# A decoder layer on one core: three stages of the attention steps in another order

## The reference

```python
qkv = x @ W_qkv
ret = einsum('bhtd,bhsd->bhts', q, k) * decay
r = einsum('bhts,bhsd->bhtd', ret, v) + cross
x = layernorm(x + group_norm(r))
# cross attention, q from x, k and v from the context
scores = where(causal, einsum('bhqd,bhkd->bhqk', q, k) * scale, -inf)
x = layernorm(x + (softmax(scores) @ v) @ Wo.T + bo)
# experts
probs = softmax(x @ router_w.T); two largest, renormed
x = layernorm(x + sum_e combine_e * (gelu(x @ w_fc[e] + b_fc[e]) @ w_proj[e] + b_proj[e]))
```

## Time and profile before

| | |
|---|---|
| median of 3 runs | 986.08 us (985.74 to 988.63) |
| span of the profiled execution | 984.6 us |
| PE busy / PEld busy | 923.6 us (94%) / 821.1 us (83%) |
| DVE busy / ACT busy / POOL busy | 663.6 us (67%) / 607.6 us (62%) / 381.9 us (39%) |
| mean granted TensorE clock | 0.979 |

### The profile page before, as it was taken

The page is one execution under the profiler, slowest core; times in us unless marked ns, Lnnn a source line. Parts: engine busy times, 40 slices in busy tenths (PEclk is TensorE's granted clock), DMA queues, the critical chain, the costliest instruction groups (busy, mean ns, idle before and its releaser), DMA issues.

```text
span 984.6 us, 29858 instructions
## 1 busy us (share of the span) xinstructions
PE 923.6 (94%) x10845; PEld 821.1 (83%) x10845; DVE 663.6 (67%) x1977; ACT 607.6 (62%) x1531; POOL 381.9 (39%) x639
## 2 busy tenths in 40 slices
PE   6899999999999999999987999999999999999950
PEld 4788888888888888888777999999999999999950
DVE  4577787777877877877744677575755775665536
ACT  4556656656556666666556566576765675665536
POOL 0224554555544656555524422222222223222223
PEclk9999999999999999999989999999999999999985
DMA  8111141111111111113012552523434433523228
GB/s 280 50 34 57 61 142 45 56 56 66 56 46 44 63 59 61 51 54 110 29 34 50 120 139 44 139 45 67 120 57 130 100 83 57 131 43 48 43 48 325
DMA packets 57361, 79.90 MB, mean 81 GB/s; under 512 B 5728, under 2 KB 46048, under 8 KB 57120
## 3 DMA queue, kind: packets, MB, share of 16 engines
q1 hardware_dynamic: 41504, 58.50, 18.1%
q0 software_dynamic: 13536, 18.16, 10.6%
q10 hardware_dynamic: 2208, 1.73, 0.6%
HBM read 52.10 MB, written 29.71 MB: 83 GB/s over the span
## 4 chain that ended last, share of the span: by engine, by line
PE 79%; ACT 7%; DVE 5%; issue 4%; DMA 2%; SPq 1%; POOL 1%; ACTq 0%; another core or an unknown queue 0%; DVEq 0%; POOLq 0%
PE bank L828 16%; PE bank L842 11%; PE bank L511 11%; PE bank L844 5%; PE bank L647 4%; PE bank L673 4%; PE bank L573 3%; PE bank L718 3%; PE bank L694 3%; PE bank L626 3%; PE bank L598 3%; PE bank L593 2%; ACT h_f L1171 2%; PE bank L732 2%; ACT last_out L1243 1%
## 5 line engine op out<-in xcount | busy, mean ns | idle before, releaser
L828 PE MATMUL bank<-xs_hi,w_both 128*128 128x256 f32 x1152 | 242.2, 287 | 1.3 <-DVE xs_lo L1471 0.8
L1165 ACT ACTIVATE h_parts<-bank,bfc_s 128x256 fp32r<-128x256 f32 x288 | 139.9, 486 | 154.6 <-PE bank L828 150.5
L1721 POOL DMA_INDIRECT residual_sum<-y_w,meta_i x72 | 114.6, 1591 | 299.6 <-DVE y_w L1543 275.7
L1501 DVE TENSOR_TENSOR h_parts<-h_f,h_parts 128x256 fp32r<-128x256 f32 x288 | 121.4, 426 | 140.2 <-ACT h_f L1171 136.6
L842 PE MATMUL bank<-w_both,h_parts 128*128 128x512 f32 x544 | 200.0, 398 | 1.1 <-DVE h_parts L1501 1.1
L828 PEld LDWEIGHTS bank<-xs_hi,w_both 128*128 128x128 f32 x1152 | 191.5, 190 | 9.4 <-issue 1.6
L828 PE MATMUL bank<-xs_lo,w_both 128*128 128x256 f32 x576 | 162.9, 283 | 0.0
L844 PE MATMUL bank<-w_both,h_parts 128*128 128x256 f32 x544 | 153.1, 281 | 0.0
L1171 ACT ACTIVATE h_f<-bank,bfc_s 128x256 f32<-128x256 f32 x288 | 139.4, 484 | 3.9 <-DVE h_parts L1501 3.4
L842 PEld LDWEIGHTS bank<-w_both,h_parts 128*128 128x128 f32 x544 | 102.5, 188 | 20.0 <-DVE h_parts L1501 4.0
L828 PEld LDWEIGHTS bank<-xs_lo,w_both 128*128 128x128 f32 x576 | 109.7, 191 | 0.0
(11 more groups left out here) (186 smaller groups left out, 2138.2 us busy)
## 6 DMA issues: line engine op xcount, KB each, us to landing
rows<-sent_rows SPq DMA_DIRECT2D x37, 258.0 KB
xc_raw<-in_turned SPq DMA_DIRECT2D x32, 256.0 KB, 3.0
w_raw<-in_w_fc SPq DMA_DIRECT2D x8, 1024.0 KB
w_raw<-in_w_proj SPq DMA_DIRECT2D x8, 1024.0 KB
x_t<-in_x SPq DMA_DIRECT2D x32, 128.0 KB, 2.2
residual_sum<-x_row SPq DMA_DIRECT2D x32, 128.0 KB, 1.7
last_in<-residual_sum SPq DMA_DIRECT2D x7, 512.0 KB, 7.8
result<-last_out SPq DMA_DIRECT2D x7, 512.0 KB, 2.7
```

Of the source, the lines that this page charges most:

```text
L828: last = mm(ps_h(g, j), w[:, at:at + P], v[:, k, :], start=(n == 0), stop=(n == 3 * NCH - 1))
L1165: A(h_hi[j % 4][:, :], ps_h(g, j), ACT.Gelu_apprx_tanh, bias=bias)
L1501: V.tensor_tensor(h_lo[j % 4][:, :], h_f[j % 2][:, :], h_hi[j % 4][:, :].bitcast(f32), ALU.subtract).then_inc(s["h_split"], 1)
L1721: G.indirect_dma_start(total, bass.IndirectOffsetOnAxis(meta_i[:, half:half + 1], 0), y_w[:, half, :], None, compute_op=ALU.add)\
```

## The change

Three engines' lists are written in another order; no stage is changed, added or dropped.

```diff
--- before.py
+++ after.py
@@ -751,16 +751,16 @@
                     run(ret_scores, At(k))
                     run(att_back, At(k - 3))
                     run(x1_turn, At(k - 1))
-                    pair_run(prep_kx, k // 2)
+                    run(att_proj, At(k - 3))
                     run(qx, At(k - 1))
-                    run(att_proj, At(k - 3))
                     run(att_scores, At(k - 2))
                     run(ret_values, At(k))
                     run(rank, At(k - 4))
-                    run(max_scores, At(k - 1))
+                    pair_run(prep_kx, k // 2)
                     run(gn_mean, At(k))
                     run(y_back, At(k))
                     run(x2_turn, At(k - 3))
+                    run(max_scores, At(k - 1))
                     run(att_values, At(k - 2))
                     run(logits, At(k - 3))
                     run(prep_v, At(k + 1))
@@ -785,8 +785,8 @@
                         fc0(0)
                     run(gn_mean, At(k))
                     run(y_back, At(k))
+                    run(x2_turn, At(k - 3))
                     run(max_scores, At(k - 1))
-                    run(x2_turn, At(k - 3))
                     run(att_values, At(k - 2))
                     run(logits, At(k - 3))
                     run(prep_v, At(k + 1))
@@ -1090,7 +1090,6 @@
                     if k >= 0:
                         pair_run(x_high, (k + 2) // 2, 0)
                     run(att_back_out, At(k - 3))
-                    pair_run(kx_out, k // 2)
                     run(max_out, At(k - 2))
                     run(qx_out, At(k - 1))
                     for r in range(0, 2):
@@ -1098,6 +1097,7 @@
                     for r in range(2, 4):
                         run(att_exp, At(k - 2), r)
                     run(y_out, At(k))
+                    pair_run(kx_out, k // 2)
                     run(x2_T_out, At(k - 3))
                     run(o_out, At(k - 2))
                     run(v_out, At(k + 1))
@@ -1405,17 +1405,17 @@
                     run(put, At(k - 4))
                     run(ln2_norm, At(k - 3))
                     run(gn_moments, At(k))
+                    run(gn_centre, At(k))
                     for r in range(NT):
                         run(att_max, At(k - 1), r)
-                    run(max_twice, At(k - 1))
-                    run(gn_centre, At(k))
                     run(lg_out, At(k - 3))
                     run(ln1_stats, At(k))
+                    run(max_twice, At(k - 1))
+                    run(ln1_sum, At(k))
                     run(att_norm, At(k - 2))
-                    run(ln1_sum, At(k))
-                    run(pick, At(k - 3))
                     run(ln1_norm, At(k))
                     run(max_split, At(k - 1))
+                    run(pick, At(k - 3))
                 if odd:
                     for r in range(NT):
                         run(ret_decay, At(k), r)
```

## The result

The changed kernel takes 1032.26 us (median of 4 runs, 1028.52 to 1033.45) beside 986.93 us of the kernel before (985.74 to 988.63): a ratio of 1.047, with a 95% interval of 1.045 to 1.049. It is slower by 45.3 us. The forecast was 1025.4 us, in a range of 1008 to 1036.

What follows compares the result with a forecast made beforehand. The loop through VectorE's decay, which releases TensorE in every step, was taken as the bound. Even steps 14.5 x 2.15 = 31.2 us plus odd steps 13.5 x 0.6 = 8.1 us, together 39.3, gave 1025.4 us, range 1008 to 1036.

Steps and rivals of the forecast that it cites:

- The loop: Decay, attention scores, retention values, query-major scores, maxima, norms, next decay: lateness in it lengthens the 30.06 us pair.
- rival 3: TensorE's own work is the bound; the even steps' 0.42 us stall becomes pure gain, 979.8 us; chance 0.04.
- Odd steps, 0.6 us: Second norm's turn waits for VectorE's rank count (L1372); query-major scores, maxima and next decay 0.6 us later, bounds 0.2 and 0.7.
- Even steps, first part, 1.42 us for the maxima: Projection behind the retention values delays the query-major scores, so the maxima start at 231.13, 1.42 us later.
- The front was a tie: Even steps: retention values at 226.39 by TensorE's front, 226.43 by the decay, so the front costs and frees nothing.
- Even steps, second part, the split's wait of 1.0 us: With the pick behind it, VectorE's split waits 1.0 us for ScalarE's rounded maxima (L1039).
- Rival 1: The split doesn't wait for ScalarE: even term 1.13 instead of 2.15 us, 1010.6 us; chance 0.15.
- 2.15 was the term: Even steps: the next decay ends at 241.01, 2.15 us later than before; 14.5 times makes 31.2 us.
- half an even term: Step 2 counted as half of a full even step's 2.15 us, as it has half of the pipeline.
- half an odd term: Step 31 counted as half of an odd step's 0.6 us.
- rival 2: New TensorE waits lower the clock to 0.94 over attention's 460 us: 1035 to 1053 us; chance 0.08.
- step 2 has half of the pipeline: Term of the sum: besides 14 full even steps, 4 to 30, step 2 counts half, giving 14.5 x 2.15 = 31.2 us.

Runs made afterwards that it cites:

- decay_later: Kernel before, with VectorE's even steps making the low part of the context in front of the four decays instead of behind them: 1000.2 us, ratio 1.013.
- both_early: Kernel before, with the pick behind the next step's decays and, in odd steps, ScalarE's rounding of the maxima ahead of the turned-back attention copy: 985.6 us, ratio 0.997.
- pick_after_decay: Kernel before, with VectorE's pick moved in every step from the step's end to behind the next step's decays: 987.8 us, ratio 1.002.
- kx_front: Changed kernel, with the context key projection and its copy back in the even step's front, the second norm's turn still ahead of the scores: 1023.9 us, ratio 1.038.
- kx_behind_only: Kernel before, with projection and copy moved behind retention values and rank, output ahead of query projection; VectorE's lists and the turn left alone: 1004.0 us, ratio 1.018.
- pick_back: Changed kernel, with VectorE's pick put back in front of the first norm's output and the split in even steps: 1015.6 us, ratio 1.028.
- max_hi_first: Changed kernel, with ScalarE's rounding of the maxima ahead of the turned-back attention copy and second row copy in odd steps: 1012.0 us, ratio 1.026.
- after_old_start: Changed kernel, with the old lists for steps -1 to 3 on all three engines: 1027.3 us, ratio 1.040.
- split_projection: both_early with the context key projection cut in halves, one in the even step's front, one behind the rank, its copy behind the group's sums: 980.2 us, ratio 0.991.
- even_only: Changed kernel, with TensorE's odd list undone, so only the even steps' lists of three engines are changed: 1023.5 us, ratio 1.037.
- odd_turn_only: Kernel before, with only the second norm's turn put ahead of the query-major scores in odd steps: 997.6 us, ratio 1.010.

## Why the prediction was right, point by point

**The loop.** Right in what it was used for, and too strong in its words. A decay that comes later is paid in full (0.82 of 0.85 us in decay_later). But "the decay on VectorE releases TensorE in every step" holds only for the odd steps; there both_early brings the decay 0.3 us forward and the retention values and the step's end with it. In the even steps decay and TensorE's own front came out within 0.14 us of each other, which pick_after_decay shows with 2.62 us in place of 1.62 and no gain. The equal 1.63 and 1.62 of the earlier trace rows were a bound in one kind of step and a tie in the other, and no row that I laid out could tell them apart. Rows that I left out could. The attention scores of the kernel before, in the steps 13 and 14:

```profile
208.47 1.31 PE L673 MATMUL bank<-qx_own,kxT 32*128 32x256 f32 x15
...
224.11 1.27 PE L673 MATMUL bank<-qx_own,kxT 32*128 32x256 f32 x16
```

In the odd step the retention values start 210.44 - 208.47 = 1.97 us behind them, in the even step 225.83 - 224.11 = 1.72: only the odd step's scores are held up, by 0.25 us. My rival 3 (979.8 us) used the same distances as its point of decision; it fell, since nothing the change does brings the front and the decay forward together.

**Odd steps, 0.6 us.** Measured 0.72 us a pair; the wait for L1372 is there with 0.34 us before each turn. The handoff that I put at "some hundredths" is the difference: the turn starts 218.84 - 218.69 = 0.15 us behind the end of VectorE's row.

**Even steps, first part, 1.42 us for the maxima.** The front was a tie as laid out: TensorE waits 1.26 us for ScalarE's copy, and the retention values start 247.06 - 245.44 = 1.62 us behind the decay. The scores start 250.78 - 245.44 = 5.34 us behind the decay's end, 5.51 were laid out (229.72 - 224.21). The mean follows 1.51 us behind the projection's start as laid out; the projection starts 3.13 instead of 3.20 us behind the decay, and the scores 0.70 instead of 0.80 us behind the mean. The maxima start 6.75 us behind it, 6.92 laid out.

What I had wrong is whose 1.51 us these are. I priced the projection as work that the loop must carry. In kx_front it is not there, TensorE waits 1.18 us for the group's sums at the same place, and the pair is only 0.08 us shorter. I never laid out when these sums are ready. The size came out because the projection is hardly longer than the wait that it covers, and that was luck: the moved scores, which now stand behind the mean, cost this first microsecond with or without the projection. The projection costs it only when the scores stand right behind it, as in kx_behind_only.

**Even steps, second part, the split's wait of 1.0 us.** Measured 1.16 us, in 13 of 13 pairs. Rival 1 is out by pick_back, which cuts this wait to 0.41 us, and max_hi_first, which ends it; they give back 1.00 and 1.14 us a pair. From one decay's end to the next it is 262.18 - 245.44 = 16.74 us, 2.09 more than before; 2.15 was the term.

**What was missing.** 2.81 us a pair against 2.75 explains 0.8 of the 7.5 us by which the span was too short. Of the rest, 2.3 are the later first start, which the order has no part in (last section). To the steps 0 to 4 I had given half an even term for step 2 (1.1 us) and of step 4 the 1.05 us by which TensorE's next step starts later, 2.1 together; they took 5.9, so 3.7 are missing there. To the stretch behind step 31 I had given 1.4 us, half an odd term and the split's wait of step 30; it took 2.0, so 0.6 are missing. In the first steps the order made the difference, as after_old_start shows, and the granted clock was lower there. The windows of the kernel before and then of the changed one, from 10 to 20, 20 to 35 and 35 to 50 us (length, busy by engine, clock, DMA share, GB/s):

```profile
10.00:20.00 10.00, 7.34 (x58) 6.36 (x57) 2.95 (x5) 4.48 (x10) 0.00 (x0) 0.90 1.06 367
20.00:35.00 15.00, 11.68 (x171) 9.90 (x170) 7.43 (x16) 6.38 (x17) 5.20 (x10) 1.00 0.33 100
35.00:50.00 15.00, 13.08 (x238) 10.88 (x237) 8.14 (x20) 8.84 (x23) 3.10 (x7) 1.00 0.03 10
```

```profile
10.00:20.00 10.00, 7.47 (x33) 6.85 (x32) 1.96 (x3) 3.51 (x6) 0.00 (x0) 0.50 1.06 358
20.00:35.00 15.00, 11.67 (x125) 9.62 (x124) 6.96 (x15) 5.38 (x14) 5.26 (x10) 0.85 0.32 95
35.00:50.00 15.00, 12.72 (x167) 10.35 (x171) 9.54 (x21) 7.85 (x22) 3.08 (x7) 0.83 0.07 21
```

That is rival 2 in a small way: not in the steady steps, whose clock stayed at 1.00, but in the first ones. A lower clock comes with such a loss also where the projection stays in front: both_early, at 0.93 and 0.85 in the last two of these windows, takes 69.5 us from the first retention scores to step 5, while pick_after_decay, with the same list for TensorE, and split_projection, which has all moves of both_early, take 64.9 and 64.6 at 1.00. So how the missing 3.7 us divide between the new waits and the clock is open. The term of the sum that was mis-sized is "step 2 has half of the pipeline": it gave the steps 0 to 3 1.1 us, and they took 4.7. The 2.0 us behind the start of step 31 come with a clock of 0.85 between 519 and 575 us, where the kernel before had 0.94 in its drain; they are within what this stretch varies from run to run, and their cause stays open.

## What to carry to other kernels

In a software pipeline written out by hand, a full TensorE row says nothing about slack: set the starts of one stage beside the ends of its inputs, step by step, and follow the loop. Equal distances mean either a bound or a tie: look whether the stage that waits is itself drawn out, and let a run that makes the input earlier and one that makes it later tell which. A stage that looks like filler may be the cover of a wait on another engine, and when it is moved, the wait comes out where it stood; where it goes it is paid again, unless a wait stands there that it can cover. Before a moved stage is priced, look up when the inputs of the stage behind it are ready. Count the first and last steps of a pipeline apart, since a cover that is spare in the steady state may be the only one there.

## What the runs showed of the hardware

*The start.* Up to 17 us all these kernels run the same list, and yet the first retention scores start either at 17.7 to 17.9 us (the kernel before, both_early, even_only, kx_behind_only) or at 19.6 to 20.3 us (the changed kernel and the eight others). TensorE's pace makes the difference. In the early group the second and third block of twelve projection matmuls (L511, 256 columns) take 0.13 us from one matmul to the next, in the late group 0.23 us. Two blocks of twelve at 0.1 us each are the 2.3 us. The windows from 12 to 15 us of the kernel before and of odd_turn_only hold the same twelve matmuls:

```profile
12.00:15.00 3.00, 1.68 (x12) 1.48 (x12) 0.00 (x0) 1.10 (x3) 0.00 (x0) 0.98 1.04 366
```

```profile
12.00:15.00 3.00, 2.70 (x12) 2.63 (x12) 0.00 (x0) 0.24 (x1) 0.00 (x0) 1.00 1.04 364
```

The changed kernel has the slow pace with a granted clock of 0.50 in this window, the 1.2 GHz level. odd_turn_only has the same pace, and its clock is given as 1.00. So this column can't be trusted in the first microseconds of a profile; the pace of equal matmuls can. Both groups hold kernels of both orders (even_only and kx_behind_only in the early one, odd_turn_only and pick_after_decay in the late one), so the 2.3 us at the start are no effect of the order.

*The end.* From the start of step 31 on, where nearly all instructions stand in the same order in all of them, it takes 505.3 to 512.3 us to the end. So the 2.0 us at the end need not be an effect of the order. The four runs of the changed kernel, whose times go from 1028.52 to 1033.45 us, have mean clocks from 0.973 down to 0.965.

*Waits and the clock.* In the steady steps of the changed kernel TensorE had a wait of 1.3 us in each even step and kept 1.00 throughout. What made the clock fall in the first steps is not settled. The five kernels with the whole projection behind from the first step on show 0.86 between 35 and 60 us and take 70.9 to 73.0 us from the first retention scores to step 5. The other eight take 64.6 to 69.5 us; five of them (the kernel before, after_old_start, odd_turn_only, pick_after_decay, split_projection) show 1.00, but both_early, which leaves the projection in front, shows 0.91 in that stretch, and kx_front and decay_later 0.93.

*VectorE beside GpSimd.* An operation of VectorE on one column took 1.78 us while GpSimd worked on 512 columns, and 0.16 us without such a neighbour (both_early). Why is not shown; in all eight steps from 21 to 28 it took 1.43 us or more.
